# Attention in one fused transformer kernel: the products with the values in plain fp32, one head in each half of the array's columns

## The reference, cut to what matters

```python
q = (xn @ Wq).reshape(b, n, H, DH).transpose(0, 2, 1, 3) * scale
kv = xn @ Wkv
k, v = (kv[..., :DH], kv[..., DH:])
...
sim = jnp.einsum('bhid,bjd->bhij', q, k)
sim = sim + bias
...
attn = jax.nn.softmax(sim, axis=-1)
out = jnp.einsum('bhij,bjd->bhid', attn, v)
out = out.transpose(0, 2, 1, 3).reshape(b, n, INNER)
out = out @ Wo
```

## Time and profile before

| | |
|---|---|
| median of two runs | 1051.87 us (1050.03, 1053.71) |
| span of the profiled execution | 1055.2 us |
| busy: PE / PEld / DVE / ACT / POOL | 88 / 77 / 76 / 70 / 57% |
| attention stage (first transposes to last projection) | about 62 to 616 us |

### The profile page before, as it was taken

How to read it: one execution, slowest core, us unless ns; L and a number is a source line. 1 busy time by engine, 2 the same in 40 slices (tenths; PEclk the granted TensorE clock), 3 DMA queues, 4 the chain that set the end, 5 groups by cost and what they waited for, 6 DMA issues and landing times. The chain is left out here.

```text
span 1055.2 us, 22432 instructions
## 1 busy us (share of the span) xinstructions
PE 932.6 (88%) x6180; PEld 811.6 (77%) x6180; DVE 803.2 (76%) x2324; ACT 735.9 (70%) x1651; POOL 606.0 (57%) x699
## 2 busy tenths in 40 slices
PE   7899999999999999999999966887976762599997
PEld 5578888888888898998888755677964652499996
DVE  7579989899898898998888879774757786344443
ACT  2268888888888998998999937434764652466663
POOL 2368777777776666775555525481066277344444
PEclk8879999999999999999999986888988885699999
DMA  9156656666666566675665440155864523254453
GB/s 309 44 175 180 189 171 189 178 181 180 176 184 182 170 197 182 187 199 167 182 189 171 137 150 1 51 167 148 282 178 157 205 102 138 88 78 78 73 84 48
DMA packets 111427, 162.14 MB, mean 154 GB/s; under 512 B 16201, under 2 KB 85193, under 8 KB 110282
## 3 DMA queue, kind: packets, MB, share of 16 engines
q1 hardware_dynamic: 100200, 140.56, 45.1%
q0 software_dynamic: 10224, 18.00, 8.2%
q10 hardware_dynamic: 882, 2.14, 0.6%
HBM read 110.31 MB, written 25.17 MB: 128 GB/s over the span
## 5 line engine op out<-in xcount | busy, mean ns | idle before, releaser
L2375 POOL TENSOR_SCALAR probs<-probs,inv_sum 128x1024 f32<-128x1024 f32 (+3 forms) x128 | 301.7, 2370 | 174.2 <-DVE inv_sum L2526 174.2
L2421 ACT ACTIVATE probs<-probs,neg_max 128x1025 f32<-128x1025 f32 (+7 forms) x256 | 197.5, 772 | 30.9 <-DVE neg_max L2486 29.8
L2508 DVE TENSOR_TENSOR pT_lo<-t_ps,pT_hi 128x512 fp32r<-128x512 f32 (+1 forms) x320 | 202.5, 633 | 21.3 <-ACT pT_hi L2403 20.8
L2590 PE MATMUL t_ps<-ident,probs 128*128 128x128 f32 x1152 | 179.9, 274 | 1.1 <-DVE pT_lo L2508 1.1
L2610 PE MATMUL o_ps<-pT_hi,values 128*128 128x256 f32 x576 | 175.0, 323 | 5.2 <-DVE pT_lo L2508 3.5
L2403 ACT ACTIVATE pT_hi<-t_ps 128x512 fp32r<-128x512 f32 (+1 forms) x320 | 175.5, 549 | 5.5 <-PE t_ps L2590 2.3
L2486 DVE CUSTOM_DVE_ANT_0 probs<-s_ps,bias_set,neg_null 128x512 f32<-128x512 f32 (+3 forms) x256 | 164.2, 642 | 4.5 <-PE s_ps L2559 2.6
L2590 PEld LDWEIGHTS t_ps<-ident,probs 128*128 128x128 f32 x1152 | 141.9, 141 | 31.4 <-DVE pT_lo L2508 2.7
L2611 PE MATMUL o_ps<-pT_lo,values 128*128 128x256 f32 x576 | 150.4, 281 | 0.0
L2558 PE MATMUL s_ps<-k_hi,q_hilo 128*128 128x512 f32 (+3 forms) x384 | 143.8, 375 | 4.2 <-PEq L2730 1.4
L2559 PE MATMUL s_ps<-k_lo,q_one 128*128 128x512 f32 (+3 forms) x384 | 135.4, 353 | 0.0
(11 more groups left out here) (385 smaller groups left out, 2124.7 us busy)
## 6 DMA issues: line engine op xcount, KB each, us to landing
bias_set<-bias_dram SPq DMA_DIRECT2D x16, 1024.0 KB, 5.5
bias_set<-bias_dram SPq DMA_DIRECT2D x16, 896.0 KB, 5.4
bias_set<-bias_dram SPq DMA_DIRECT2D x16, 768.0 KB, 4.9
bias_set<-bias_dram SPq DMA_DIRECT2D x16, 640.0 KB, 4.7
q_hilo<-q_hi SPq DMA_DIRECT2D x128, 64.0 KB, 2.0
q_hilo<-q_lo SPq DMA_DIRECT2D x128, 64.0 KB, 2.0
q_one<-q_hi SPq DMA_DIRECT2D x128, 64.0 KB, 2.0
bias_set<-bias_dram SPq DMA_DIRECT2D x16, 512.0 KB, 5.5
```

Source lines behind the costliest of these rows:

```text
L2375: last = pool.tensor_scalar(keys, keys, inv_sum[:, x.set, unit, h:h + 1], None, ALU.mult)
L2421: act.activation(p, p, ACT.Exp, scale=-1.0, bias=neg_max[:, x.set, row.unit, h:h + 1], accum_out=row_sum[:, x.set, row.unit, h:h + 1]).the ...
L2508: dve.tensor_tensor(pT_lo[n % 3][:, 0:count, :], t_ps[TURNS["slot", n] % 3][:, 0:2 * P * count].rearrange("p (n q) -> p n q", n=count), pT ...
L2590: last = pe.transpose(t_ps[at % 3][:, P * (2 * m + h):P * (2 * m + h) + P], probs_row(x, row, h)[:, 1 + P * (k + m):1 + P * (k + m) + P], ...
```

## The change

`pT_hi` and `pT_lo` become one plain fp32 tile `pT`, `values` keeps 64 columns in fp32, and the product of each head with the values is a matmul of its own, with 64 weight columns and 128 moving columns: head 0 writes partitions 0 to 63 of `o_ps`, head 1 partitions 64 to 127. `o_ps` is then laid out as `oT` is, and one copy takes it over. The copy out of `t_ps` is done by ScalarE in slots 0 to 2 of a step and by VectorE in slots 3 and 4, each on its own; the semaphores follow.

```diff
+ACT_SLOTS = 3
...
-        self.pT_hi = [sbuf(st, f"pT_hi{i}", [P, 2, 2 * P], F32R) for i in range(3)]
-        self.pT_lo = [sbuf(st, f"pT_lo{i}", [P, 2, 2 * P], F32R) for i in range(3)]
+        self.pT = [sbuf(st, f"pT{i}", [P, 2, 2, P]) for i in range(3)]
         self.oT = [sbuf(st, f"oT{i}", [P, P]) for i in range(2)]
-        self.o_low = [sbuf(st, f"o_low{i}", [DH, 2 * P]) for i in range(2)]
...
-        o_ps = [psum(st, f"o_ps{i}", [P, CW])[:, 0:2 * P] for i in range(2)]
+        o_ps = [psum(st, f"o_ps{i}", [P, CW])[:, 0:P] for i in range(2)]
...
+        def by_act(n):
+            return n % SLOTS_A_STEP < ACT_SLOTS
+
+        def copied(pe, n):
+
+            g, i = divmod(n, SLOTS_A_STEP)
+            if by_act(n):
+                pe.wait_ge(act_out, ACT_SLOTS * g + i + 1)
+            else:
+                pe.wait_ge(dve_out, (SLOTS_A_STEP - ACT_SLOTS) * g + i - ACT_SLOTS + 1)
+
+        def bank_free(pe, at):
+
+            if at < 3:
+                return
+            kind, n = TURN_AT[at - 3]
+            if kind == "null":
+                pe.wait_ge(null_out, n + 1)
+            else:
+                copied(pe, n)
...
-                def high(n):
-                    if n >= NS:
+                def copy_out(n):
+                    if n >= NS or not by_act(n):
                         return
                     x, i = slot_of(n)
                     row, k, count = x.slots[i]
                     wait(act, pv_done, n - 2)
                     act.wait_ge(turn_ready, n + 1)
-                    act.activation(pT_hi[n % 3][:, 0:count, :], t_ps[TURNS["slot", n] % 3][:, 0:2 * P * count], ACT.Copy).then_inc(hi_out, 1)
-
-                def outputs(x, row):
-                    wait(act, oT_ready, units_done(x.g, row.unit) - 2)
-                    act.wait_ge(pv_done, SLOTS_A_STEP * x.g + (len(x.rows[0].slots) if row.unit == 0 else SLOTS_A_STEP))
-                    act.activation(o_low[row.unit][:], o_ps[row.unit][DH:P, :], ACT.Copy).then_inc(o_low_ready, 1)
+                    act.activation(pT[n % 3][:, 0:count], t_ps[TURNS["slot", n] % 3][:, 0:2 * P * count].rearrange("p (n h q) -> p n h q", n=count, h=2),
+                                   ACT.Copy).then_inc(act_out, 1)
...
-                    dve.wait_ge(hi_out, n + 1)
-                    dve.tensor_tensor(pT_lo[n % 3][:, 0:count, :], t_ps[TURNS["slot", n] % 3][:, 0:2 * P * count].rearrange("p (n q) -> p n q", n=count),
-                                      pT_hi[n % 3][:, 0:count, :].bitcast(F32), ALU.subtract).then_inc(t_read, 1)
+                    if not by_act(n):
+                        wait(dve, pv_done, n - 2)
+                        dve.wait_ge(turn_ready, n + 1)
+                        dve.tensor_copy(pT[n % 3][:, 0:count], t_ps[TURNS["slot", n] % 3][:, 0:2 * P * count].rearrange("p (n h q) -> p n h q", n=count, h=2)
+                                        ).then_inc(dve_out, 1)
...
-                    dve.wait_ge(o_low_ready, units_done(x.g, row.unit))
-                    for h in range(2):
-                        cols = slice(P * h, P * h + P)
-                        last = dve.tensor_tensor(oT[row.unit][DH * h:DH * h + DH, :], o_ps[row.unit][0:DH, cols], o_low[row.unit][:, cols], ALU.add)
-                    last.then_inc(oT_ready, 1)
+                    dve.wait_ge(pv_done, SLOTS_A_STEP * x.g + (len(x.rows[0].slots) if row.unit == 0 else SLOTS_A_STEP))
+                    dve.tensor_copy(oT[row.unit][:], o_ps[row.unit]).then_inc(oT_ready, 1)
...
-                    wait(pe, t_read, at - 2)
+                    bank_free(pe, at)
...
-                    pe.wait_ge(t_read, TURNS["slot", n] + 1)
+                    copied(pe, n)
                     for m in range(count):
-                        v = values[:, QT * x.batch + k + m, :]
-                        pe.matmul(o_ps[row.unit], v, pT_hi[n % 3][:, m, :], start=(k + m == 0), stop=False)
-                        last = pe.matmul(o_ps[row.unit], v, pT_lo[n % 3][:, m, :], start=False, stop=(k + m == row.blocks - 1))
+                        for h in range(2):
+                            last = pe.matmul(o_ps[row.unit][DH * h:DH * h + DH, :], values[:, QT * x.batch + k + m, :], pT[n % 3][:, m, h, :],
+                                             start=(k + m == 0), stop=(k + m == row.blocks - 1), skip_group_check=True)
                     last.then_inc(pv_done, 1)
...
-        values = sbuf(attn, "values", [P, NT, P], F32R)
+        values = sbuf(attn, "values", [P, NT, DH])
...
-                        dve.tensor_tensor(values[:, rows, DH:P], vps[g % 2][:, :, 0:DH], values[:, rows, 0:DH].bitcast(F32), ALU.subtract)
```

More of the change, by code:

```diff
@@ L2189 @@
         TURNS["null", _n // (SLOTS_A_STEP * PAIRS)] = len(TURNS)
+TURN_AT = list(TURNS)
 EXPS_AT = {n: [] for n in range(-1, NS + 1)}
@@ L2281, in attention_stage @@
         null_wT = tiles.null_wT
-        pT_hi = tiles.pT_hi
-        pT_lo = tiles.pT_lo
+        pT = tiles.pT
         oT = tiles.oT
-        o_low = tiles.o_low
         s_ps = [psum(st, f"s_ps{i}", [P, CW]) for i in range(2)]
         t_ps = [psum(st, f"t_ps{i}", [P, CW]) for i in range(3)]
-        o_ps = [psum(st, f"o_ps{i}", [P, CW])[:, 0:2 * P] for i in range(2)]
+        o_ps = [psum(st, f"o_ps{i}", [P, CW])[:, 0:P] for i in range(2)]
         y_ps = psum(st, "y_ps", [P, 2, D])
@@ L2295, in attention_stage @@
         marks_act = sem("marks_act")
-        turn_ready, hi_out, t_read, pv_done = sem("turn_ready"), sem("hi_out"), sem("t_read"), sem("pv_done")
-        oT_ready, o_low_ready, projected, null_turned, y_ready, y_out = (
-            sem("oT_ready"), sem("o_low_ready"), sem("projected"), sem("null_turned"), sem("y_ready"), sem("y_out"))
+        turn_ready, act_out, dve_out, null_out, pv_done = (
+            sem("turn_ready"), sem("act_out"), sem("dve_out"), sem("null_out"), sem("pv_done"))
+        oT_ready, projected, null_turned, y_ready, y_out = (
+            sem("oT_ready"), sem("projected"), sem("null_turned"), sem("y_ready"), sem("y_out"))
         marks_sp, marks_pool, marks_dve = sem("marks_sp"), sem("marks_pool"), sem("marks_dve")
@@ L2446, in _ @@
                 normalise_short(0)
[L2447 to L2454, removed]
+                copy_out(0)
+                for n in range(NS):
+                    copy_out(n + 1)
                     for item in SCORES_AT[n]:
@@ L2500, in fill, with copy_out @@
                         scores(item[1], item[2])
-                def low(n):
+                def copy_out(n):
                     if n >= NS:
@@ L2513, in low @@
                         wait(dve, y_ready, r - 1)
-                        dve.tensor_copy(null_wT[r % 2][:], t_ps[TURNS["null", r] % 3][0:H, 0:2 * P]).then_inc(t_read, 1)
+                        dve.tensor_copy(null_wT[r % 2][:], t_ps[TURNS["null", r] % 3][0:H, 0:2 * P]).then_inc(null_out, 1)
                 def outputs(x, row):
                     wait(dve, projected, units_done(x.g, row.unit) - 2)
-                    dve.wait_ge(o_low_ready, units_done(x.g, row.unit))
-                    for h in range(2):
-                        cols = slice(P * h, P * h + P)
-                        last = dve.tensor_tensor(oT[row.unit][DH * h:DH * h + DH, :], o_ps[row.unit][0:DH, cols], o_low[row.unit][:, cols], ALU.add)
-                    last.then_inc(oT_ready, 1)
+                    dve.wait_ge(pv_done, SLOTS_A_STEP * x.g + (len(x.rows[0].slots) if row.unit == 0 else SLOTS_A_STEP))
+                    dve.tensor_copy(oT[row.unit][:], o_ps[row.unit]).then_inc(oT_ready, 1)
                 def invert(x, row):
@@ L2531, in _ @@
                         invert(ALL[item[1]], ALL[item[1]].rows[item[2] == 5])
-                low(0)
+                copy_out(0)
                 for n in range(NS + 1):
@@ L2535, in _ @@
                         fill(item)
-                    low(n + 1)
+                    copy_out(n + 1)
                     for item in SCORES_AT.get(n, ())[1:]:
@@ L2621, in project @@
                     if x.pair == PAIRS - 1 and row.unit == 1:
-                        pe.wait_ge(t_read, TURNS["null", x.round] + 1)
+                        pe.wait_ge(null_out, x.round + 1)
                         for unit in range(2):
@@ L2765, in values_high @@
                         act.wait_ge(v_ready, g + 1)
-                        act.activation(values[:, 4 * g:4 * g + 4, 0:DH], vps[g % 2][:, :, 0:DH], ACT.Copy).then_inc(v_out, 1)
+                        act.activation(values[:, 4 * g:4 * g + 4, :], vps[g % 2][:, :, 0:DH], ACT.Copy).then_inc(v_out, 1)
                     def first_query(g):
```

## The result

The changed kernel takes 1115.23 us, median of two runs (1114.75 and 1115.71), against 1051.87: a ratio of 1.0585, 95% interval 1.0542 to 1.0628.

The account below looks back on a forecast made before the run. TensorE was taken to bound the stage. Products +0.37, switches +1.73 and waits -0.40 gave +1.70 us a step, x 64 = +109 on 1051.9: some 1160 us, range 1120 to 1250.

Parts of the forecast that it names:

- The bound and the place: TensorE bounds the stage, 8.02 of 8.55 us a step; nothing behind the stage changes.
- The switches, +1.73 us a step: TensorE entering and leaving the split array around each value-product group: 5 a step at 0.345 us; bounds 0 and 1.9.
- Rivals 2 and 3: Switching the array costs nothing: halves side by side, 1017 us, 14%; or serial, 1138 us, 8%.
- rival 4: Half the switch cost hidden in existing waits, or paid only one way: 1105 to 1135 us, 8%.
- The products, +0.37 forecast: Value products on TensorE: side by side but started in program order, 2.50 us a step against 2.13.
- The figure of 0.22 a block: Lower bound for a block's value products, both heads side by side: 2 x 0.11 us.
- The waits, -0.40 forecast: TensorE's waiting of 0.53 us a step: about 0.4 goes, as copies no longer pass through two engines in turn.
- The upper bound of 0.53: Most that TensorE's waits could shrink, in us a step: all the waiting counted in the kernel before.
- a step of 10.1 us: Sign: step length of the changed kernel, read from the projections, against 8.55 us before.
- VectorE and ScalarE were to fall to 5.3 and 5.6 us a step: Sign: busy time in the stage, from 7.6 and 7.5 us, some 52% and 55% of a 10.1 us step.
- The wait of the score loads for part_max: Sign: TensorE's loads waiting for VectorE's score read, 31 times, 7.7 us in all, must go.

Follow-up runs that it names:

- e_one_half: Changed kernel with both heads' value products in the lower half of the array's columns, and two copies of a row's outputs: 1243.42 us, ratio 1.1774.
- e_headmajor: Changed kernel with a two-block slot's value products reordered, both blocks of the first head, then both of the second: 1117.84 us, ratio 1.0585.
- e_light_copies: TensorE's products as in the kernel before (fp32r, full width, no switches) with the changed kernel's copies; result incomplete: 1028.0 us, ratio 0.9783.
- e_all_dve: Changed kernel with all five copies of a step on VectorE (ACT_SLOTS = 0): 1120.43 us, ratio 1.061.
- e_query_late: Changed kernel with one group of value products a step, row outputs copied before the next score, query products right ahead of the group: 1065.99 us, ratio 1.0103.
- e_full_width: Changed kernel in plain fp32 without the split: values twice in 128 weight columns, one 256-column product a block, two output copies: 1135.95 us, ratio 1.0744.
- e_groups9: Changed kernel with each two-block slot's value products in two groups, one ahead of the transposes, nine groups a step not five: 1192.2 us, ratio 1.1335.

## Why the prediction was wrong

**The bound and the place.** Right. TensorE's own work sets the step, the loss lies wholly between the first and the last projection, nothing moved behind the stage, and the clock held.

**The switches, +1.73 us a step.** Right in mechanism and in size: 5 x 0.343 = 1.72, from rows of a 16-column product outside the stage. The open load of 64 columns was estimated at 0.055 between the 16- and the 128-column one; the first values' record holds the next one up by some 0.05. Rivals 2 and 3 (no switch cost) and 4 (half of it hidden or paid one way) fell. The measured 1115 lies in rival 4's 1105 to 1135, but by chance: the switch is paid in full, both ways. The Trainium skill's sentence that a change of the tiling mode drains the engine ("TensorEngine Tiling (Array Packing)", Key Properties) holds here, with a gap of 0.093 us ahead of the load each way. The prediction tied the switch to outputs in partitions 64 to 127; e_one_half shows it without them.

**The products, +0.37 forecast.** This is the step that failed. Side by side was right, but the term rested on the sentence that records start in program order, so that each group begins and ends with one half alone. They come in full pairs: 18 pairs x 0.109 = 1.96, against 2.13, so the term is -0.17, with another sign. That is 0.54 x 64 = 35 of the 45 us. e_headmajor shows why: the halves don't wait for each other. The figure of 0.22 a block stood in the text as a bound. With it and the other terms as forecast the sum is some 1126, still inside the range; the waits did the rest. The reason given for side by side, that operands and banks share nothing, was not so: both heads read the same weights and write the same bank, in different partitions. They ran side by side all the same.

**The waits, -0.40 forecast.** Too small by 0.15, which is the other 10 of the 45 us. TensorE's own work is 8.02 before and 8.02 - 2.13 + 1.96 + 1.72 = 9.57 after. The last steps have no scores and queries left to do (two and four steps), which takes about 0.13 off both means: 7.89 and 9.44. The measured 8.55 and 9.55 leave 0.66 and 0.11 us: 0.55 went. (The null column's products at the rounds' ends are not in these sums; they are the same in both kernels.) The upper bound of 0.53 in the text was short, since it set the mean of 63 steps against a full step's work. e_light_copies puts 0.35 of it on the copies, close to the 0.4. The other 0.2 is gone only in the changed kernel. That its longer step absorbs them is likely, since e_all_dve hides 1.6 us of further work in its slack, but not shown; the 0.2 was not traced to single waits.

**The sum with the measured terms.** -0.17 + 1.72 - 0.55 = +1.00 us a step, x 64 = 64; measured are 63.4. The forecast's +1.70 was 109.

**The smaller signs.** The prediction gave a step of 10.1 us as a sign, but its own sum makes 8.55 + 1.70 = 10.25; measured are 9.55. VectorE and ScalarE were to fall to 5.3 and 5.6 us a step; they fell to 5.6 and 6.0 (58.5 and 63.2% of 9.55, from 260 to 360 us). The wait of the score loads for part_max was to go. The profile lists 8.2 us in 47 waits for part_max and 7.2 in 42 for neg_max, against 7.7 in 31 for part_max before, but 88 of those 89 are the gap of 0.17 on the way out of the split: the load at 305.18 has it like the one at 303.94, and the profile puts the one down to neg_max and the other to no engine. One is a longer wait, 0.33. So this sign came true.

**Can it be mended?** One group a step is the least that there can be. It adds 0.34 and the pairs save 0.17, so TensorE's work stays 0.17 us a step above the kernel before. e_query_late, the best of these, is 1.0% slower than that kernel (0.5 to 1.5%). Its step is 8.80 us, of which 9.44 - 4 x 0.343 = 8.07 are TensorE's own work by the sums above; the other 0.73 is about the waiting of the kernel before, 0.66. So an order of work with one group and fewer waits could still be faster; none was found here. None of the kernels that compute the full result beat the kernel before.

## What to carry to other kernels

Count how often a kernel changes between the full array and a split one, not only how much faster the split products are: here each round trip costs 0.34 us on an engine that is the bound, as much as three fp32 records of 128 columns, and one rare product elsewhere in the trace gave that price ahead of time. It is the narrow weights that bring it: with the values padded to 128 weight columns (e_full_width) there is none. Before such switches are grouped, look at what the engine behind TensorE does meanwhile: a group of 2.2 us without scores left VectorE idle and then gave it all its work at once, and cost more than the switches saved until the row outputs and projections were moved forward. And a gain on engines that are not the bound is worth only the waits that they cause, here 23 us (e_light_copies).

## What the runs showed of the hardware that was not expected

Two plain fp32 products in different halves of the array's columns run fully side by side, 0.109 us for two records of 128 columns (e_one_half: 0.109 for one), even when four records of one half stand ahead of the other half's first (e_headmajor). The open weight load on the way out of the split depends on what comes: 0.107 ahead of a score product, 0.057 ahead of transposes with as many weight columns (e_groups9). And the two transposes with 16 weight columns show neither the gap nor the open load, though the plain product with 16 does; in the changed kernel too they are 0.11 us from the records on either side.
